# Layer operands loaded in twelve pieces of 128 KB, and the result stored in four

## The reference

```python
def _gat_layer(h, mask, b):
    scores = jnp.einsum('...nd,...md->...nm', h, h)
    scores = jnp.where(mask, scores, NEG)
    attn = jax.nn.softmax(scores, axis=-1)
    return jnp.einsum('...nm,...md->...nd', attn, h) + b

h = jnp.einsum('bnc,hdc->bhnd', x, Wh)
out_h = _gat_layer(h, mask[None, None], bh[None, :, None, :])     # 32 instances: layer 1
z = jax.nn.leaky_relu(transposed and joined heads of out_h, 0.2)
h2 = jnp.einsum('bnk,dk->bnd', z, Wo)
out2 = _gat_layer(h2, mask[None], bo)                             # 8 instances: layer 2
z2 = jax.nn.leaky_relu(out2, 0.2), then its layer norm
```

## Time and profile before

| | us |
|---|---|
| median of 3 timed runs | 3159.49 |
| the three runs | 3157.59, 3159.53, 3159.49 |
| the profiled execution, its time | 3153.17 |
| its span, first to last instruction | 3150.7 |
| PE matmul busy | 2944.5 (93%) |
| VectorE busy | 2695.5 (86%) |
| ACT busy | 2286.1 (73%) |
| GpSimd busy | 2551.7 (81%) |

### The profile page before, as it was taken

The page is one execution under the profiler, slowest core; times in us unless marked ns, Lnnn a source line. Parts: engine busy times, 40 slices in busy tenths (PEclk is TensorE's granted clock), DMA queues, the critical chain, the costliest instruction groups (busy, mean ns, idle before and its releaser), DMA issues. The chain is left out here.

```text
span 3150.7 us, 124706 instructions
## 1 busy us (share of the span) xinstructions
PE 2944.5 (93%) x49505; PEld 2174.7 (69%) x49505; DVE 2695.5 (86%) x5566; ACT 2286.1 (73%) x2670; POOL 2551.7 (81%) x1439
## 2 busy tenths in 40 slices
PE   6868899999999999999999999999999889999990
PEld 4436677777777777777777777777777867777770
DVE  6766788888888888888888888898887579999997
ACT  2238677777777777777777777777777567777773
POOL 1147699999999999899999999998998269888882
PEclk8989999999999999999999999999999999999995
DMA  6209789999999998999889999899987978998872
GB/s 218 72 1 368 187 156 163 168 163 160 158 164 169 164 160 159 160 167 167 159 156 163 169 164 159 158 164 168 166 158 125 320 150 154 162 163 161 158 142 88
DMA packets 1443659, 514.20 MB, mean 163 GB/s; under 512 B 1359182, under 2 KB 1416972, under 8 KB 1441036
## 3 DMA queue, kind: packets, MB, share of 16 engines
q1 hardware_dynamic: 1443212, 507.32, 82.9%
HBM read 105.27 MB, written 66.06 MB: 54 GB/s over the span
## 5 line engine op out<-in xcount | busy, mean ns | idle before, releaser
L559 POOL TENSOR_TENSOR low<-probs 128x1024 f16<-128x1024 f32 x1280 | 2397.1, 1895 | 349.9 <-ACT probs L851 243.3
L851 ACT ACTIVATE probs<-scores,shifted_max 128x2048 f32<-128x2048 f32 x640 | 1282.4, 2004 | 219.3 <-DVE shifted_max L1055 216.1
L716 PE MATMUL ps<-operands 128*128 128x512 f16 x2560 | 973.1, 380 | 9.3 <-DMA v_parts<-h_d 6.7
L717 PE MATMUL ps<-operands 128*128 128x512 f16 x2560 | 972.7, 380 | 0.0
L1050 DVE CUSTOM_DVE_ANT_0 scores<-ps,mask,neg_max 128x1024 f32<-128x1024 f32 x640 | 821.6, 1284 | 126.3 <-issue 85.9
L879 ACT COPY probsT<-ps 128x1024 bf16<-128x1024 bf16 x640 | 647.6, 1012 | 379.6 <-PE ps L725 375.8
L725 PEld LDWEIGHTS ps<-ident,probs 128*128 128x128 bf16 x10240 | 651.5, 98 | 373.4 <-issue 204.2
L1050 DVE CUSTOM_DVE_ANT_0 scores<-ps,mask 128x1024 f32<-128x1024 f32 x640 | 781.5, 1221 | 132.1 <-PE ps L717 123.1
L725 PE MATMUL ps<-ident,probs 128*128 128x128 bf16 x10240 | 781.9, 219 | 12.4 <-DVE probsT L1064 7.5
L735 PE MATMUL ps<-v_parts,probsT 128*128 128x64 f16 x10240 | 685.7, 193 | 8.0 <-issue 6.3
L736 PE MATMUL ps<-v_parts,probsT 128*128 128x64 f16 x10240 | 686.0, 193 | 0.0
(11 more groups left out here) (156 smaller groups left out, 1802.3 us busy)
## 6 DMA issues: line engine op xcount, KB each, us to landing
operands<-hT_d SPq DMA_DIRECT2D x40, 512.0 KB, 4.4
operands<-hT_d SPq DMA_DIRECT2D x80, 256.0 KB, 4.3
v_parts<-h_d SPq DMA_DIRECT2D x40, 512.0 KB, 4.7
probsT<-low SPq DMA_TRANSPOSE x1280, 3.6
z_d<-outs SPq DMA_DIRECT2D x38, 512.0 KB, 3.6
scores<-in_adj SPq DMA_DIRECT2D x16, 1024.0 KB, 4.7
h_d<-probs SPq DMA_DIRECT2D x32, 512.0 KB, 6.1
hT_d<-probsT SPq DMA_DIRECT2D x32, 512.0 KB, 5.5
```

Source lines behind the costliest of these rows:

```text
L559: pool.tensor_tensor(low[:, u, w], probs[:, u, w], high[:, u, w], ALU.subtract).then_inc(sem(f"low{half}"), 1)
L716: pe.matmul(ps[:, b, :], hi_lo[:, p, t * P:(t + 1) * P], hi_lo[:, p, w], start=True, stop=False)
L717: scored = pe.matmul(ps[:, b, :], hi_lo[:, p, t * P:(t + 1) * P], lo_hi[:, p, w], start=False, stop=True)
L851: act.activation(probs[:, 1 - u, :], scores[:, 1 - u, :], ACT.Exp, bias=shifted_max[:, 1 - u:2 - u], scale=-1.0, accum_out=row_sum[:, held ...
```

## The change

The four loads of an instance become twelve of 128 KB each: `hi_lo` in four pieces of 512 columns over 128 partitions, each half of `lo_hi` in two pieces of 1024 columns over 64 partitions, `v_parts` in four pieces of 512 columns. One is issued in each of steps 1 to 12, in place of one in each of steps 3 to 6. The wait before the first is now for `scores1` (PE has made all scores of the instance before), and the waits for `high_weighed` and `weighed` stand before the first piece of `v_parts`, in step 9. The store of a result becomes four stores of 128 KB, in steps 0, 1, 3 and 7 of the following instance instead of step 10; each waits for its own group of four tiles. Counts in waits follow. The loads at the start of a layer and the last store of layer 1 are cut in the same way, all pieces in a row.

```diff
-OPERAND_DMAS = 4
+OPERAND_DMAS = 12
...
             def load_part(i, parity, k):
 
                 s = sem(f"operands{parity}")
-                if k == 3:
-                    sp.dma_start(v_parts[:, parity, :], h_d[:, i, :] if isinstance(i, int) else h_d[:, bass.ds(i, 1), :]).then_inc(s, 16)
+                if k >= 8:
+                    w = slice((k - 8) * 4 * P, (k - 7) * 4 * P)
+                    sp.dma_start(v_parts[:, parity, w], h_d[:, i, w] if isinstance(i, int) else h_d[:, bass.ds(i, 1), w]).then_inc(s, 16)
                     return
-                to, row, at, rows_ = ((hi_lo, 0, 0, P), (lo_hi, 0, D, D), (lo_hi, D, 0, D))[k]
+                if k < 4:
+                    to, row, at, rows_, w = hi_lo, 0, 0, P, slice(k * N // 4, (k + 1) * N // 4)
+                else:
+                    to, row, at, rows_, w = lo_hi, (k - 4) // 2 * D, D - (k - 4) // 2 * D, D, slice(k % 2 * N // 2, (k % 2 + 1) * N // 2)
                 at = i * P + at
-                sp.dma_start(to[row:row + rows_, parity, :],
-                             hT_d[at:at + rows_, :] if isinstance(i, int) else hT_d[bass.ds(at, rows_), :]).then_inc(s, 16)
+                sp.dma_start(to[row:row + rows_, parity, w],
+                             hT_d[at:at + rows_, w] if isinstance(i, int) else hT_d[bass.ds(at, rows_), w]).then_inc(s, 16)
...
-            def store_z(i, p, base=0):
-                sp.wait_ge(sem("out_copied"), i * 4 + 4)
+            def store_z(i, p, k, base=0):
+                sp.wait_ge(sem("out_copied"), i * 4 + k + 1)
                 gate(sp, "sp")
-                sp.dma_start(z_d[:, i - base, :] if isinstance(i, int) else z_d[:, bass.ds(i - base, 1), :], outs[:, p, :]).then_inc(sem(f"z_stored{p}"), 16)
+                w = slice(k * 4 * D, (k + 1) * 4 * D)
+                sp.dma_start(z_d[:, i - base, w] if isinstance(i, int) else z_d[:, bass.ds(i - base, 1), w], outs[:, p, w]).then_inc(sem(f"z_stored{p}"), 16)
...
-                k = t - 3
+                k = t - 1
                 if 0 <= k < OPERAND_DMAS and not (isinstance(i, int) and i in (0, LAYER1 - 1, LAYER1, INSTANCES - 1)):
                     if k == 0:
+                        sp.wait_ge(sem("scores1"), i * NT)
+                        gate(sp, "sp")
+                    if k == 8:
                         sp.wait_ge(sem("high_weighed"), i * NT)
...
-                if t == 10 and not (isinstance(i, int) and i in (0, LAYER1, INSTANCES - 1)):
-                    store_z(i - 1, 1 - p, LAYER1 if second else 0)
+                if t in (0, 1, 3, 7) and not (isinstance(i, int) and i in (0, LAYER1, INSTANCES - 1, INSTANCES)):
+                    store_z(i - 1, 1 - p, (0, 1, 3, 7).index(t), LAYER1 if second else 0)
...
-            store_z(LAYER1 - 1, 1)
+            for k in range(4):
+                store_z(LAYER1 - 1, 1, k)
```

More of the change, by code:

```diff
@@ L421, in load_y @@
             def load_y(b):
-                sp.wait_ge(sem(f"z_stored{b % 2}"), 8 * (LAYER1 + b - b % 2) + 16)
+                sp.wait_ge(sem(f"z_stored{b % 2}"), 32 * (LAYER1 + b - b % 2) + 64)
                 sp.dma_start(y_of(b), z_d[:, b, :]).then_inc(sem(f"y_loaded{b}"), 16)
@@ L455, in _ @@
             for b in range(4):
-                sp.wait_ge(sem(f"z_stored{b % 2}"), 16 * (b // 2 + 1))
+                sp.wait_ge(sem(f"z_stored{b % 2}"), 64 * (b // 2 + 1))
             sp.wait_ge(sem("exp_done"), LAYER1 * NT)
@@ L464, in _ @@
             for u in range(2):
-                sp.wait_ge(sem(f"z_stored{u}"), 8 * LAYER1)
+                sp.wait_ge(sem(f"z_stored{u}"), 32 * LAYER1)
             quads(sp, p2_step)
@@ L860, in tile_step @@
                     if k == 0:
-                        since(act, sem(f"z_stored{held}"), (old - held) * 8)
+                        since(act, sem(f"z_stored{held}"), (old - held) * 32)
                     act.copy(z_halves(held, k, 0), by_tile(group_bank(k))).then_inc(sem("out_high"), 1)
@@ L1075, in tile_step @@
                         gate(dve, "dve")
-                        since(dve, sem(f"z_stored{held}"), (old - held) * 8)
+                        since(dve, sem(f"z_stored{held}"), (old - held) * 32)
                     gate(dve, "dve")
```

## The result

The changed kernel takes 3162.01 us in the median (3156.19 to 3171.89, 20 runs) against 3157.01 for the kernel before measured with it (3152.85 to 3164.16, 20 runs): a ratio of 1.0019, 95% interval 1.0012 to 1.0026. It is slower by 0.19%, 5 us. The forecast was 3149.2 and faster; 3162 lies inside the range that it gave (3142 to 3163), but on the other side of the kernel before. In a second comparison the changed kernel was slower by 0.35% (1.0035, interval 1.0022 to 1.0047).

What follows compares the result with a forecast made beforehand. TensorE (PE) was taken as the bound, so only its waits cost time. The terms -11.8 + 1 + 1 - 0.5 = -10.3 us took 3159.49 to 3149.2 us, with a range of 3142 to 3163.

Steps and rivals of the forecast that it cites:

- PE sets the pace, and the loads make it wait by late landings: Whole kernel: only what makes PE wait costs time; its waits for DMA transposes, 13.6 us, lie behind the loads.
- Packets of 1 KB cost 1% more DMA time: DMA engines, steady state: four small packets take 180 ns against 163 for a large one, 0.55 us more in 65.5.
- SP's queue: Steady state: 1.6 us free a tile, so one load fits with 0.8 left; steps 1, 3, 7 just about fit.
- A later transpose costs nothing while landings are below the limit: Transposes in 12 tiles of 16 start 0.3 us later, at no cost while landings stay 1 us below some 6.
- Four fifths of 14.8 us gained: Stalls in both layers: 13.6 to 16.0 us available, four fifths of the middle taken as gain, -11.8 us.
- Moved waits cost nothing: Waits for scores1, weighed and the store's groups, at new steps: cost 0, the store having 2.8 us in hand.
- Rival D: SP waits for VectorE at a store's piece, with transposes behind it; +11 us, 3171; chance 0.03.
- Starts: Starts of layer 1 and layer 2, loads cut: +1 us each, from ranges 0.4 to 2 and 0 to 3.
- Between the layers, -0.5: Last store of layer 1: SP's 3.1 us wait for it shortens by 0.94 if on the path; -0.5 taken.
- Rival C: Later transposes in twelve tiles instead of four, a tenth passing 6 us and stalling; about +9, 3168; chance 0.08.
- Rival B: No difference: late landings come from transposes' bunching and other traffic, half the stalls remain; -3, 3156 (3153 to 3164); chance 0.27.
- A: The forecast itself: spread loads no longer make PE wait; 3149 us (own range 3143 to 3153); chance 0.62.

## Why the prediction was wrong, step by step

- *PE sets the pace, and the loads make it wait by late landings.* Right. With the loads alone cut or spread, the waits at tiles 6 and 8 go (one of 0.1 us is left); layer 2 gained 4.5 us of the 3.4 to 5.8.
- *Packets of 1 KB cost 1% more DMA time.* Right: in 700:2300 the packets of loads and stores hold the engines 12.2% of the time, 11.3% before. The share as a whole went from 0.93 to 0.92 in the first half of it, and with the issues on ACT the same pieces made the kernel faster.
- *SP's queue.* This is the step that failed. It set free time to 4.09 - 2 x 1.24 = 1.6 us a tile, from the median issue of a transpose in a quiet stretch. The trace of before gave the free time directly, 251.6 us in 391 tiles: 0.64. Of the 1.0 us between them, 0.4 are in the transposes, whose mean is 1.42 us (1113.1 us for 782) as some issues block (up to 3.9 us), 0.2 are the loads and stores that stand there already, and 0.4 are other instructions of SP and the gaps between them. The prediction held the added issue at up to 0.83; it is 0.73. With 0.64 for 1.6 the sum reads: tiles 0 to 12 have 13 x 0.64 = 8.3 us free, and 11 x 0.83 = 9.1 are added there by the prediction's own price (8.0 by the measured one). Nothing is left, and steps 1, 3 and 7 with two issues run over. The trace of before said so without any experiment.
- *A later transpose costs nothing while landings are below the limit.* Wrong in its terms: the limit holds for lag and landing together. Landings never passed 5.5 us in the stretch, and PE's waits in it rose from 6.4 to 10.9 us. "Landings within 5.5 in every tile" came true for the 448 tiles and showed nothing. The other signs that were named failed: 93 issues of a transpose in the 28 instances took 2 us or more (78 before), PE's waits were 21.8 us in place of under 4, and an instance 65.75 in place of 65.3.
- *Four fifths of 14.8 us gained.* In layer 1 it was a loss of 5.0 in place of a gain of 7.6, and that is 12.6 of the 15.3 us by which the forecast missed; the gain was there and was taken back at tiles 5, 9 and 12 (12 of 20 waits stand there in the second trace). The experiment with the store whole in step 14 has it, 8 us.
- *Moved waits cost nothing.* Right. In the changed kernel SP waited for outs 3.0 us in 2 waits over the whole kernel, before 3.6 in one, at the end of layer 1. Rival D, with SP held up by the store's wait, is out.
- *Starts.* For layer 2 0 to +1.3 was expected; PE waits 7.30 us in place of 6.72. PE's timeline of the changed kernel:

```profile
2548.03 0.61 PE L725 MATMUL ps<-operands 128*128 128x512 f16 x1 [7.30 <-DMA v_parts<-h_d]
```

  For layer 1 the first instance took 71.06 and 68.50 us in the two traces (68.79 before); no cost can be told from that. All that lies outside the 28 and 6 instances had +1.5 in the forecast; it grew by 11.1 and 4.2 us in the two traces. So the term of the seams was perhaps too small as well.
- *Between the layers, -0.5.* The sign is doubtful: the pieces stand behind four loads of 512 KB, and SP waits 6.0 and 4.4 us in the two traces for their landing, before 3.1. SP's waits, 2440:2475, changed kernel:

```profile
SPq L474 <- DMA z_d<-outs: 6.0, 1, 6.0
```

- *The rivals.* Rival C, slower by later transposes in twelve tiles, comes nearest to the mechanism of layer 1 (it had +9; 0.19% and 0.35%, 5 to 11 us, were measured), with a chance of 0.08. Its point of decision was put in landings above 6 us, of which there was none in the 448 tiles, and not in SP's free time, and so looked far away. Rival B had the time in its range (3153 to 3164), but not by its reason: its sign was that landings stay at 6 us. Its dearer starts may be part of the truth. That 3162 lies in the forecast's whole range is owed to B and says nothing for A.
- *The rule for large transfers.* The Trainium skill, page "DMA: Bandwidth & Descriptors", section "Bandwidth", advises large transfers, and the kernel did get slower. The estimate from that page, 22 us an instance by 2.0 us of the engines for each added DMA, does not describe it: the share of the engines did not rise, and a DMA more cost 0.73 us of the queue that issues it. With the pieces' issues placed otherwise the kernel is faster than before, so the rule doesn't decide here.

What is not settled is why some steps bear a whole load and others don't. In the trace of the changed kernel all 187 transpose issues in the 28 instances that took over 1.45 us had a 16 KB packet of the instruction queue within 2.5 us, against some 60% of the short ones, and these packets come in nearly the same tiles of the two-instance loop body each time. In the run with loads in 1, 4, 7 and 10 such a packet starts within some 0.5 us of the load of step 10 in every odd instance, and 3.2 to 4.4 us behind it in every even one; 13 of the 14 odd instances stalled there and no even one. (The two packets in a row at tiles 11 and 12, of which the text on record speaks, stand in the even ones.) In the run with that load in step 13 none starts within 2.7 us of it, and there is no stall. This fits, but it is argued and not shown; no run moved the fetches.

## What to carry to other kernels

Before adding issues to a queue, read its free time from the wait that ends it (here SP waiting for GpSimd) and set it against the number of added issues in the fullest stretch, each with its whole price; a median of issue times overstates what is free. Limits on a hand-over belong to the sum of lag (from the data being ready to the issue) and landing. Moving a few large transfers apart, into steps that bear them, gave more (12 us) than cutting them into twelve (0 alone, 8 with the store moved), with no issue added; which steps bear them had to be tried (one choice gave 0, one 12).

## What the runs showed of the hardware

- An added DMA costs SP 0.73 us of free time in the changed kernel, while its own issue record is 0.53 on average (205.4 us for 389); the rest is other instructions of SP and gaps between them. Eleven of 8 KB were not cheaper (0.73 too) than the change's pieces of 128 KB. Over the runs the price was 0.66 to 0.80, and 1.06 where only the store was cut.
- The issue of a DMA transpose took 1.23 us at the least in the earlier trace rows and blocked SP for up to 3.9.
- Sixteen DMA engines with a share of 0.92 took 33,000 more packets in 1600 us (872400 against 839635 on the queue) without a fuller share.
- Loads on ACT's queue beside transposes on SP's: PE's waits for the transposes were 0.8 us in 1600, with landings over 5.5 us in 9 tiles.
